# An LSTM and a UGRNN layer over 128 steps: one scan per step in place of two, with the cell state in SBUF

## The reference, cut to what matters

```python
# layer 0: LSTM cell, once per time step
a = xw_t + prev_h @ Wh              # xw_t = x_t @ Wx + b, [32, 512]
i, f, o = sigmoid(a[:, :H]), sigmoid(a[:, H:2*H]), sigmoid(a[:, 2*H:3*H])
g = tanh(a[:, 3*H:])
next_c = f * prev_c + i * g
next_h = o * tanh(next_c)
# x = x + all next_h
# layer 1: UGRNN cell, once per time step
m = concatenate([xt, h]) @ weight + bias
c, g = tanh(m[:, U:]), sigmoid(m[:, :U] + 1.0)
h_new = g * h + (1.0 - g) * c
# x = x + all h_new
```

## Time and profile before

| what | us |
|---|---|
| median of 3 runs | 248.93 |
| lowest, highest | 247.79, 250.43 |
| the profiled execution | 247.93 |
| its span | 246.1 |
| VectorE busy in it | 224.0 |
| TensorE busy in it | 229.9 |
| ScalarE busy in it | 130.0 |

### The profile page before, as it was taken

One profiled execution on the slowest core, in us unless ns is written; L12 is line 12 of the kernel. 1 busy time (PEld: TensorE's weight loads), 2 busy tenths in 40 slices (PEclk: granted clock), 3 DMA queues, 4 the chain that ended last, 5 costly groups with the idle time before them and its releaser, 6 DMA issues.

```text
span 246.1 us, 14402 instructions
## 1 busy us (share of the span) xinstructions
PE 229.9 (93%) x5604; PEld 181.0 (74%) x5604; DVE 224.0 (91%) x1558; ACT 130.0 (53%) x907; POOL 5.6 (2%) x15
## 2 busy tenths in 40 slices
PE   3999999999999999999999999999999999999772
PEld 2777777778787787868778787787777777777672
DVE  6599999999999999999999999999999999999994
ACT  3455555555555555554555545555455555555542
POOL 1700000000000000000000000000000000000000
PEclk9999999999999999999999999999999999999955
DMA  6001010010101001010010101001010100000000
GB/s 216 22 15 39 24 45 14 24 48 13 48 21 32 21 21 43 11 43 21 15 39 21 33 20 43 21 11 43 21 32 21 43 11 21 23 13 15 17 13 11
DMA packets 12260, 7.43 MB, mean 30 GB/s; under 512 B 1478, under 2 KB 11980, under 8 KB 12236
## 3 DMA queue, kind: packets, MB, share of 16 engines
q1 hardware_dynamic: 11936, 6.82, 9.5%
q10 hardware_dynamic: 300, 0.28, 0.3%
HBM read 5.00 MB, written 2.10 MB: 29 GB/s over the span
## 4 chain that ended last, share of the span: by engine, by line
PE 69%; DVE 20%; ACT 6%; issue 3%; DMA 1%; SPq 0%; ACTq 0%
PE a L286 14%; PE fo L261 11%; PE ig L261 6%; PE fo L232 6%; PE ig L232 6%; PE a L277 5%; PE a L237 5%; PE fo L266 5%; DVE cell_bank L496 5%; PE a L280 4%; DVE h_high L503 4%; PE ig L266 4%; ACT act_bank L413 4%; DVE scan_add L489 2%; DVE h_low L508 2%
## 5 line engine op out<-in xcount | busy, mean ns | idle before, releaser
L261 PEld LDWEIGHTS fo<-h_high,wh_part 128*128 128x128 bf16 x762 | 36.4, 96 | 49.1 <-DVE h_high L503 48.8
L403 ACT ACTIVATE act_bank<-fo 128x32 f32<-128x32 f32 x128 | 23.3, 182 | 81.9 <-PE fo L266 81.1
L261 PE MATMUL fo<-h_high,wh_part 128*128 128x32 f16 x762 | 59.3, 179 | 7.5 <-DVE h_high L503 6.9
L266 PE MATMUL fo<-h_low,wh_part 128*128 128x32 f16 x508 | 52.9, 180 | 0.2 <-DVE h_low L508 0.2
L277 PE MATMUL a<-h_high,w1x_part 128*128 128x32 f16 x768 | 45.1, 177 | 0.8 <-DVE h_low L508 0.8
L280 PE MATMUL a<-h_low,w1x_part 128*128 128x32 f16 x512 | 41.9, 177 | 0.0
L496 DVE TENSOR_TENSOR_SCAN cell_bank<-scan_mul,scan_add 128x64 f32<-128x64 f32 x128 | 38.7, 303 | 0.7 <-ACT scan_add L407 0.3
L286 PE MATMUL a<-acts,w1h_part 128*128 128x32 bf16 x768 | 38.7, 177 | 0.0
L261 PE MATMUL ig<-h_high,wh_part 128*128 128x32 f16 x762 | 38.3, 177 | 0.0
L409 ACT ACTIVATE out_gate<-fo 128x32 f32<-128x32 f32 x128 | 25.2, 197 | 20.6 <-PE fo L266 20.6
L277 PEld LDWEIGHTS a<-h_high,w1x_part 128*128 128x128 bf16 x768 | 34.8, 96 | 0.9 <-ACT acts L419 0.9
(11 more groups left out here) (80 smaller groups left out, 489.6 us busy)
## 6 DMA issues: line engine op xcount, KB each, us to landing
xT<-in_x_dram SPq DMA_DIRECT2D x16, 128.0 KB, 2.1
x_add<-in_x_dram SPq DMA_DIRECT2D x32, 64.0 KB, 1.8
out_dram<-outT SPq DMA_DIRECT2D x32, 64.0 KB, 1.6
wx_s<-in_L_cond_Wx_dram SPq DMA_DIRECT2D x1, 256.0 KB, 2.9
wh_raw<-in_L_cond_Wh_dram ACTq DMA_DIRECT2D x1, 256.0 KB, 3.2
w_raw<-in_L_cond_weight_dram SPq DMA_DIRECT2D x1, 256.0 KB, 4.1
bias_rows<-in_biases_dram ACTq DMA_DIRECT2D x1, 3.0 KB
condT<-in_cond_dram ACTq DMA_DIRECT2D x1, 16.0 KB, 3.9
```

The lines of the kernel that those rows point to most:

```text
L261: nc.tensor.matmul(gate_step(q, j), wh_part[:, w, q * P:(q + 1) * P], h_high[:, (j - 1) % PARTS, :], start=False, stop=False, skip_group_c ...
L266: mm = nc.tensor.matmul(gate_step(q, j), wh_part[:, w, q * P:(q + 1) * P], h_low[:, (j - 1) % PARTS, :], start=False, stop=w == 1, skip_gr ...
```

## The change

The second scan of a step is taken out. `cell` is now a tile in SBUF with the shape that `cell_kept` had; the one scan writes it, ScalarE's tanh (line 413 before) reads it there, and so does the product of the next step (line 489). The PSUM bank `cell_bank` and the semaphore `kept_ready`, for which nothing waited, go. All other instructions and their order stay.

```diff
-        cell_kept = sb("cell_kept", [P, N, 2])
+        cell = sb("cell", [P, N, 2])
...
-        cell_bank, act_bank = bank("cell_bank"), bank("act_bank")
-        cell = cell_bank[:, 0:2 * N].rearrange("p (n two) -> p n two", two=2)
+        act_bank = bank("act_bank")
...
-            nc.vector.memset(cell_kept[:, :, :].rearrange("p n two -> p (n two)"), 0.0).then_inc(cell_zero, 1)
+            nc.vector.memset(cell[:, :, :].rearrange("p n two -> p (n two)"), 0.0).then_inc(cell_zero, 1)
...
-                nc.vector.tensor_tensor(scan_add[:, :, 1], forget[:, :], cell_kept[:, :, 1],
+                nc.vector.tensor_tensor(scan_add[:, :, 1], forget[:, :], cell[:, :, 1],
                                         ALU.mult).then_inc(scan_in_ready, 1)
...
-                for to, done in ((cell, cell_ready), (cell_kept, kept_ready)):
-                    nc.vector.tensor_tensor_scan(to[:, :, :].rearrange("p n two -> p (n two)"),
-                                                 scan_mul[:, :, :].rearrange("p n two -> p (n two)"),
-                                                 scan_add[:, :, :].rearrange("p n two -> p (n two)"),
-                                                 0.0, ALU.mult, ALU.add).then_inc(done, 1)
+                nc.vector.tensor_tensor_scan(cell[:, :, :].rearrange("p n two -> p (n two)"),
+                                             scan_mul[:, :, :].rearrange("p n two -> p (n two)"),
+                                             scan_add[:, :, :].rearrange("p n two -> p (n two)"),
+                                             0.0, ALU.mult, ALU.add).then_inc(cell_ready, 1)
```

More of the change, by code:

```diff
@@ L112, in two_layer_recurrence @@
         f_ready, tanh_c_ready, cell_ready = sem("f_ready"), sem("tanh_c_ready"), sem("cell_ready")
-        kept_ready = sem("kept_ready")
         scan_in_ready = sem("scan_in_ready")
```

## The result

| what | before | after |
|---|---|---|
| median, us | 248.34 | 250.19 |
| lowest, highest, us | 247.59, 250.79 | 249.6, 252.42 |
| ratio to before, 95% interval | | 1.0076 (1.005 to 1.0101) |
| span of the profiled execution, us | 246.1 | 248.2 |

The kernel became slower by 0.8%, some 1.9 us: inside the bound of 1% that was set for "no change", and clear of zero. 249.7 had been forecast, against a median of before that was then 248.93. In both kernels 5 of the 20 executions took some 2.3 us longer than the rest (250.2 to 250.8 before, 252.2 to 252.4 after), so a median of four or six executions further down depends on how many of them were such.

What follows compares the result with a forecast made beforehand. The prediction took a loop of latencies, 1.81 us a step, as the bound, not an engine's throughput. Scan -26 and tanh +32 gave +6 ns a step, +0.8 us on 248.93: 249.7 us, range 246.6 to 252.6.

Steps and rivals of the forecast that it cites:

- A loop of latencies: Waits from h_high through matmuls, sigmoid, scan_add, scan and tanh back to h_high fill the 1.81 us step; change priced on scan and tanh.
- The second scan lies under the tanh: Scan into cell_kept ends at 123.12, before tanh ends at 123.17; removing it frees 34 us of VectorE, costed at nothing.
- The scan into SBUF: VectorE's remaining scan: 265 + 8 = 273 ns instead of 299, a gain of 26 ns a step, 18 at least.
- a pair of one form: VectorE lines 521 (waits, 192 ns) and 548 (doesn't, 184), both SBUF to SBUF, taken to price a scan's waiting.
- The tanh out of SBUF: ScalarE's tanh reading the cell from SBUF instead of PSUM: 214 ns instead of 182, a cost of 32 ns a step.
- my two estimates of 16 and 32: Extra ns for ScalarE's SBUF read: 32 from instructions after a stand or table change, 16 from copies following without a wait.
- two separate rows both give 229: ScalarE SBUF-to-SBUF instructions, 128x1 in 203 ns and 128x128 in 309, interpolated at 0.835 ns a column to 32 columns.
- The sum: Scan and tanh on the loop: -26 + 32 = +6 ns a step, x 127 = +0.8 us.
- the likeliest case: No change worth measuring: scan gain and tanh loss cancel within some 19 ns, 247.4 to 251.0 us; chance 0.70.
- The late instruction: VectorE scan in one early step, late with 0.27 us idle put down to issue; could move, 0.3 us either way once.
- The faster rival: Scan gains its full 34 ns, tanh loses 14 or less: net -20 ns a step, -2.5 us, 246.4; chance 0.08.
- The slower rival: ScalarE's SBUF read costs more than the scan's write saves: +38 ns a step, +4.8 us, 253.7; chance 0.20.

## Why the prediction was right, point by point

- **A loop of latencies, not an engine, sets the period.** Right, and shown: one scan less in each step, 23 us of VectorE's busy time, gave a ratio of 1.0005. Also right were the place of the two links that count, and that the gaps of 0.03 to 0.04 would stay.
- **The second scan lies under the tanh.** Right, shown from both sides: put back it doesn't help, taken out alone it doesn't hurt. The busy time forecast with it, 190 us, was wrong: it was 200.7, since I subtracted the whole 265 ns of a scan that overlaps the one before it.
- **The scan into SBUF, 273 ns, -26.** Mis-sized: 292, -7. The step that failed is "what waiting adds is seen on a pair of one form". I took the 8 ns between lines 521 and 548 for a scan, where waiting adds 26. I kept 18 as the least gain; it was 7, outside my own bound. I had priced a surcharge by another operation although the size of this one was open between 0 and all 34. The prediction had named a scan still near 300 as a sign that waiting made the first one long; with 292 that sign came: waiting is 25 to 27 of the 34 ns, PSUM 7 to 9.
- **The tanh out of SBUF, 214 ns, +32.** Right in direction, too high: 203, +21, between my two estimates of 16 and 32. The reason that I gave for the higher one, that waiting shows in full, was right (203 against 183), but the copies of other widths at the start overstated it. My "two separate rows both give 229" was no second witness either: a line drawn through two points gives the same value from both ends. The rows at the start would put a 32-column SBUF to SBUF instruction at 229, while 203 and the 15 ns between lines 413 and 409 give 218. Whether that comes from the width or from the function (copy, sigmoid) was not tried.
- **The sum.** +6 ns forecast, +14 measured; both terms were too large, by 19 and 11, and their errors partly cancelled. 1.8 us instead of 0.8. The net of +14 lies within the -12 to +16 given for the likeliest case, and the direction was right; the period, 1.823, lies outside the "1.815 at most". That 249.7 came so near to 250.19 is in part luck: it started from a median of before that was 0.6 above that of the twenty executions. From 248.34 the forecast would have been 249.1.
- **The late instruction, left out of the sum.** It did move, as was said: from 0.72 to 0.88 us over the loop, +0.16, within the 0.3 given for it. That and a start that came 0.1 us later make up most of what 1.8 leaves of the span's 2.1.
- **The faster rival and the rule behind it.** The Trainium skill (Perfetto Trace Analysis, section Optimizing Scalar/DVE Operations) gives VectorE 65 ns less on SBUF than on PSUM and ScalarE 42 more. For VectorE the trace doesn't agree: a scan's destination is worth 7 to 9 ns, and a source in PSUM costs nothing (of the products that wait, 192 with one operand in PSUM, line 489, and 192 with none, line 527; of those that don't, 180, line 505, and 184, line 540). For ScalarE it agrees in one place: from the start of the waiting tanh to the start of line 414 it is now 0.14 us, with PSUM 0.09. The page calls its figures engine-busy times, and this distance is one. But on the chain only 21 ns of it count, since the next link waits for the end of the tanh and not for ScalarE to be free. Measurement decides, and the rival falls.
- **The slower rival** needed a tanh price of 46; it was 21.

## What to carry to other kernels

On a loop of latencies, price an instruction by a row of the same operation in the same state: one that waits for its input, or one that follows at once. The two can differ by 26 ns, more than the choice of memory (7 to 9 ns for VectorE's write, 21 for ScalarE's read, 15 for its write). A duplicate that gives each reader the memory it reads at the lower price can be free where the engine stands idle for a wait behind it; cutting busy time there saves nothing.

## What was not expected of the hardware

- Waiting adds 25 to 27 ns to the recorded duration of a 128x64 scan in either memory, 8 to a 128x32 product, 20 to a ScalarE tanh out of SBUF, and 2 at most to ScalarE out of PSUM (`out_gate`, which waits, 197; line 407, which doesn't, 195).
- One VectorE instruction more ahead of the loop removed late instructions inside it worth 0.9 us in the kernel after, and 0.5 of 0.7 us in the kernel before; the same one behind the loop removed none. The large late one was the 320th entry of VectorE's stream in all eight traces that show it at full size.
